# A one-core gated-attention and mixture-of-experts kernel: row weights travel with the scattered rows, expert 1 is split in phase one, and the mixing stage is rearranged

## What is computed

```python
x = x + layernorm(attention(layernorm(x)))        # state S = g_t * S + k_t v_t, y_t = q_t S
def swiglu(x, w1, w2, w3): h = x @ w1; return h * sigmoid(h) * (x @ w2) @ w3      # 256 -> 512 -> 256
gate_out = xn @ gate_w                            # 8 columns; top 2 are taken
w = softmax over the two largest, 0 elsewhere
out = sum_e swiglu(xn, ew1[e], ew2[e], ew3[e]) * w[:, e] + swiglu(xn, sw1, sw2, sw3)
x = x + layernorm(out)
```

## Time and profile before

| what | value |
|---|---|
| median of 3 runs (lowest, highest) | 833.86 us (831.44, 841.46) |
| the profiled execution's own time | 839.79 us |
| its span, first to last instruction | 837.9 us |
| mean granted PE clock | 0.953 |
| busy: PE, DVE, POOL, ACT | 87%, 66%, 61%, 49% |

### The profile page before, as it was taken

How to read it: one execution, slowest core, us unless ns; L and a number is a source line. 1 busy time by engine, 2 the same in 40 slices (tenths; PEclk the granted TensorE clock), 3 DMA queues, 4 the chain that set the end, 5 groups by cost and what they waited for, 6 DMA issues and landing times. The chain is left out here.

```text
span 837.9 us, 25066 instructions
## 1 busy us (share of the span) xinstructions
PE 732.9 (87%) x8863; PEld 609.9 (73%) x8863; DVE 551.6 (66%) x1130; ACT 408.4 (49%) x793; POOL 507.4 (61%) x672
## 2 busy tenths in 40 slices
PE   5889988898999878287999999999999999998970
PEld 4677776776877766165878999999999866887750
DVE  4999999888998886375777544444444434468852
ACT  3656655555666653222334444444444445445551
POOL 4133346776687676578098877886663444258864
PEclk9999999899999999587999999999999999999995
DMA  7435333443335433796212221212222122148864
GB/s 250 103 79 123 91 116 88 145 116 116 116 118 143 122 114 107 247 310 229 62 27 52 65 77 59 60 51 91 77 84 58 53 65 66 56 134 177 179 147 50
DMA packets 56934, 92.70 MB, mean 111 GB/s; under 512 B 7184, under 2 KB 35216, under 8 KB 56816
## 3 DMA queue, kind: packets, MB, share of 16 engines
q1 hardware_dynamic: 39424, 59.61, 25.4%
q0 software_dynamic: 11216, 23.10, 10.1%
q10 hardware_dynamic: 6176, 8.40, 3.1%
HBM read 59.07 MB, written 32.01 MB: 109 GB/s over the span
## 5 line engine op out<-in xcount | busy, mean ns | idle before, releaser
L1260 PE MATMUL bank<-xh,W 128*128 128x256 f16 x1504 | 261.8, 275 | 20.0 <-DVE gl L1556 13.8
L1260 PE MATMUL bank<-xl,W 128*128 128x256 f16 x752 | 206.8, 275 | 3.3 <-issue 3.3
L1260 PEld LDWEIGHTS bank<-xh,W 128*128 (+1 forms) x1504 | 148.2, 99 | 47.0 <-issue 16.7
L1301 PE MATMUL bank<-W,gh 128*128 (+1 forms) x824 | 142.3, 277 | 5.8 <-DVE gl L1556 3.9
L1339 ACT ACTIVATE gh<-bank 128x512 f16<-128x512 f32 x103 | 61.4, 596 | 160.8 <-DVE bank L1565 146.6
L1641 POOL DMA_INDIRECT yt_scratch<-ysh,dest x71 | 77.0, 1085 | 101.4 <-ACT ysh L1374 60.2
L1556 DVE TENSOR_TENSOR gl<-bank,gh 128x512 f16<-128x512 f32 x103 | 71.1, 691 | 73.0 <-ACT gh L1339 65.0
L1301 PE MATMUL bank<-W,gl 128*128 (+1 forms) x412 | 114.2, 277 | 0.0
L544 POOL DMA_INDIRECT xs_scratch<-xn_all,posi x64 | 92.9, 1451 | 27.5 <-issue 15.3
L1565 DVE SCALAR_TENSOR_TENSOR bank<-sl,w_scale,bank 128x512 f32<-128x512 f32 x94 | 70.9, 754 | 56.7 <-PE bank L1260 42.4
L596 PE MATMUL bank<-xnT,wT 128*128 128x256 f32 x384 | 93.6, 395 | 2.3 <-ACT xnT L371 2.3
(11 more groups left out here) (200 smaller groups left out, 1330.6 us busy)
## 6 DMA issues: line engine op xcount, KB each, us to landing
W<-gate_scratch SPq DMA_DIRECT2D x64, 256.0 KB
ysh<-yt_scratch SPq DMA_DIRECT2D x16, 512.0 KB, 4.4
xt<-xs_scratch SPq DMA_DIRECT2D x31, 260.0 KB
W<-in_L_ffn_ew_dram ACTq DMA_DIRECT2D x15, 512.0 KB, 3.8
W<-in_L_ffn_ew_dram SPq DMA_DIRECT2D x9, 512.0 KB, 9.1
x_in<-in_L_attn_x_dram SPq DMA_DIRECT2D x16, 256.0 KB, 4.0
out_dram<-x SPq DMA_DIRECT2D x16, 256.0 KB
xT_scratch<-xn2T SPq DMA_DIRECT2D x16, 256.0 KB
```

The source lines that it names most:

```text
L1260: last = mm(dst[n % 2][:, i * R:(i + 1) * R], W16[:, e, m, s, at:at + P], a[:, k, :], start=(k == 0 and s == 0 and a is x_h), stop=(k == K ...
L1301: last = mm(pYB[t.u % 2][:, r * D:(r + 1) * D], g[:, i, r, :], W16[:, e, 2, s, c * D:(c + 1) * D], start=(c == 0 and r == 0 and a is gh an ...
```

## The change

1. **Row weights.** `top` computes d per step, ACT's new `share` writes tanh(d / 2) into the fourth extra column, and POOL's `scatter` writes 0.5 - 0.5 tanh into the third. In phase two DVE's new `weights_of_rows` works out each loaded row's weight times the expert's scale, and `rows_out` evicts a routed tile with that as its scale, 256 columns at a time. `wts_all` and its computation go, and mixing becomes plain sums.
2. **Expert 1** is split by POOL in phase one in three pieces (`split_first`, steps i = 5 to 7, one matrix each), with two free `xn2` buffers as scratch.
3. **EARLY = 4**: one shared unit moves from the front to the back (routed units are 4 to 43, late shared ones 44 to 55). The table is spread over five gaps instead of three, and maxima and scales move two gaps later; `SHARE` stays.
4. ACT issues one load of an expert's matrix where it issued two.
5. **Last stage.** POOL makes the low part of late shared units' x. `add_first` is one sum of the two routed rows, `add_rows` one sum with the shared rows, behind the gated product; the normalisation moves one step later; three `lnc` buffers instead of two. The last two blocks read the shared result from PSUM; their residual is loaded by SP, added by DVE and stored by SP, without the accumulating transfer.
6. PE waits for evictions unit by unit (`rows_upto`), and projects the last singles ahead of the shared unit's hidden products.

```diff
-    EARLY = 5
+    EARLY = 4
...
+            def share(s):
+                act.wait_ge(s_dv, s + 1)
+                act.activation(xn2[s % XB][:, :, D + 3], dv[:, s], ACT.Tanh, scale=0.5).then_inc(s_share, 1)
...
             def scatter(s):
...
+                pool.wait_ge(s_share, s + 1)
                 pool.tensor_copy(xn2[s % XB][:, :, D:D + 2], tag_all[:, s]).then_inc(S["tag_ready"], 1)
-                need(pool, S["tag_ready"], s + 1)
+                pool.tensor_scalar(xn2[s % XB][:, :, D + 2], xn2[s % XB][:, :, D + 3], -0.5, 0.5, ALU.mult, ALU.add)\
+                    .then_inc(S["tag_ready"], 1)
+                need(pool, S["tag_ready"], 2 * (s + 1))
...
+            def split_first(m):
+                pool.wait_ge(s_scale, 1)
+                link(pool.tensor_scalar(spare_rows, W[:, 1, m, :], w_scale[:, 1, 1:2], 1.0, ALU.mult, ALU.mult))
+                link(pool.tensor_copy(W16[:, 1, m, 0, :], spare_rows))
+                last = pool.tensor_tensor(W16[:, 1, m, 1, :], spare_rows, W16[:, 1, m, 0, :], ALU.subtract)
...
                 on(residual, i - 2)
+                if 0 <= i - SPLIT - 1 < 3:
+                    split_first(i - SPLIT - 1)
...
+                V.tensor_tensor(dv[:, s], mx[:, s, :, 1], mx[:, s, :, 0], ALU.subtract).then_inc(s_dv, 1)
...
-                need(sp, U["mix2"], B * (c - 1))
+                need(sp, U["mix1"], c - 1)
...
+            def load_x1():
...
+                for c in PLAIN:
+                    sp.dma_start(x1_of[c], out_by_step[c]).then_inc(x1_loaded, 16)
+
+            def store_rows(c):
+                sp.wait_ge(U["sum_ready"], B * (c - PLAIN[0] + 1))
+                sp.dma_start(out_by_step[c], lnc[c % LN][:, :, :]).then_inc(last_stored, 16)
...
+                if t.routed:
+                    act.wait_ge(T["wrow_ready"], t.q + 1)
+                    for r in range(t.tiles):
+                        act.activation(ysh[:, ETILES + (t.j + r) % RING, :], pYB[t.u % 2][:, r * D:(r + 1) * D], ACT.Copy,
+                                       scale=wrow[:, t.j + r:t.j + r + 1]).then_inc(T["yo_ready"], 1)
...
-                need_dma(act, out_stored, c - 2)
+                need_dma(act, out_stored, c - LN)
...
+            TABLE = 5
...
-                turn = 3 * u + gap - 3
+                turn = 3 * u + gap - TABLE
...
+            def weights_of_rows(t, e):
...
+                dve.wait_ge(T["tag_ready"], 2 * (t.q + 1))
+                link(V.tensor_scalar(own, tag[:, t.j:t.j + t.tiles, 1], 0.0, None, ALU.is_equal))
+                link(V.tensor_tensor(part, own, x[:, 0:t.tiles, D + 3], ALU.mult))
+                link(V.tensor_tensor(part, part, x[:, 0:t.tiles, D + 2], ALU.add))
+                V.tensor_scalar(out, part, w_scale[:, 2, e], None, ALU.mult).then_inc(T["wrow_ready"], 1)
...
-                if following is not None:
+                if following is not None and u < MIX0:
                     low_x(following)
                 if prev is not None and prev.kind == "single":
                     low_g(prev, 0)
-                if steps:
-                    if steps[0] > 0:
-                        shift(steps[0] - 1)
-                    add_rows(steps[0])
+                if following is not None and following.routed:
+                    weights_of_rows(following, expert_of(dve, following))
+                if waiting is not None:
+                    shift(waiting)
                 beside(u, 0)
                 if t is not None:
                     e = expert_of(dve, t)
                     gated(t, 0, e)
                 if steps:
+                    add_rows(steps[0])
                     stats_of(steps[0])
...
+            for u in range(MIX0, ENDS):
+                if unit_at(u + 1) is not None:
+                    low_x(unit_at(u + 1))
+                for c in mixes[u]:
+                    add_first(c)
+                    if c > 0:
+                        rstd(c - 1)
+                    if c > 1:
+                        finish(c - 2)
             rstd(C - 1)
-            finish(C - 2)
-            finish(C - 1)
```

More of the change, by code:

```diff
@@ L462, in scalar_a @@
                 on(lambda s: mask_q(s, 1), i - 1)
-            act.wait_ge(s_dv, 1)
-            act.activation(ew[:, :], dv[:, :], ACT.Exp).then_inc(s_ew, 1)
         def pool_a(pool):
@@ L1132, in sandwich_kernel, with rows_upto @@
         tile_unit = {t.j + r: t for t in routed for r in range(t.tiles)}
+        def rows_upto(u):
+            return sum(t.tiles if t.routed else 1 for t in units[:u + 1])
         def halves_upto(u):
@@ L1154, in sandwich_kernel @@
         assert all(len(cs) in (1, 2) and c - EARLY + T0 + 2 <= u for u, cs in mixes.items() for c in cs)
+        PLAIN = (C - 2, C - 1)
+        x1_of = {c: xt[c % 2][:, :, 0:D] for c in PLAIN}
         def entry(eng, row, t, least, most):
@@ L1314, in tensor_b @@
                     turn_x(following)
+                late = [y for y in projected(u) if y.kind == "single" and t is not None and t.kind == "shared"]
+                for y in late:
+                    project(y, e_of.pop(y.u))
                 if t is not None:
@@ L1328, in tensor_b @@
                 for y in projected(u):
-                    project(y, e_of.pop(y.u))
+                    if y not in late:
+                        project(y, e_of.pop(y.u))
         def scalar_b(act):
@@ L1387, in load_matrices @@
             def load_matrices():
-                for e, m in [x for x in (next(matrices, None), next(matrices, None)) if x]:
+                e, m = next(matrices, (None, None))
+                if e is not None:
                     load_matrix(act, e, m)
@@ L1398, in scalar_b @@
                 t, prev, following = unit_at(u), unit_at(u - 1), unit_at(u + 1)
+                if following is not None and not following.routed:
+                    high_x(following)
                 for y in projected(u - 1):
-                    rows_out(y, e_of.pop(y.u))
+                    e = e_of.pop(y.u)
+                    if y.routed or y.n not in PLAIN:
+                        rows_out(y, e)
                 if following is not None:
-                    high_x(following)
                     e_of[u + 1] = expert_of(act, following)
                     if following.routed:
+                        high_x(following)
                         tags(following, e_of[u + 1])
                 load_matrices()
-                steps = mixes.get(u, ())
                 if t is not None:
@@ L1411, in scalar_b @@
                     high_g(prev, 0)
-                if steps and steps[0] > 0:
-                    normalise_rows(steps[0] - 1)
+                for c in mixes.get(u - 1, ()):
+                    normalise_rows(c)
                 if t is not None and t.halves == 2:
@@ L1646, in pool_b @@
             j = 0
-            for n, (first, end) in enumerate(GROUPS):
+            for n, (first, end) in list(enumerate(GROUPS))[1:]:
                 pool.wait_ge(s_scale, n + 1)
-                for e in range(max(first, 1), end):
+                for e in range(first, end):
                     split(e)
```

173 lines of the change are left out of this document (102 added, 71 removed).

## The result

The kernel after takes 878.07 us (median of 4 runs, 874.3 to 883.23), the kernel before, run beside it on the same chip, 835.82 us (4 runs, 831.44 to 841.46): ratio 1.0506, 95% interval 1.0413 to 1.0598. The prediction was 838.2 us with a range of 824 to 851; the kernel takes 40 us more. Ratios go by fast runs alone, which leaves two of the ten runs of experiment 11 out of its ratio. The profiled execution took 880.8 us (span 878.7), its counterpart before 839.8 (span 837.9).

What follows compares the result with a forecast made beforehand. DVE bounds phase one, PE the routed units at 8.30 us; +4.2 + 2.1 + 4.8 + 3.1 - 9.9 = +4.3 on 839.8 gives 844.1, carried to the median 838.2 us; range 824 to 851.

Steps and rivals of the forecast that it cites:

- the cost of the row weights in DVE's step: Routed units: four chained operations at 0.21 us and a second table read, 1.1 us a step on DVE.
- The second wait: Expert 2's first rows (fifth pair): later scales make PE wait 10 us, 45 us after the first routed rows; +2.1 us.
- Behind it: Units 7 to 9 take 10.3 us each while maxima ride, +4.8 us; then DVE's 8.0 stays under PE's 8.30.
- The signs that the prediction named for its own failure: No PE hole at expert 2's rows (forecast 10 too high), or phase one ending over 10 us later than 352 (too low).
- Phase one: Up to the handover: DVE's subtractions +2.7 and POOL's split pieces 1.5, together +4.2 us, bounds 0 and 21.
- Rival C: Phase one stretches: POOL's pieces and extra operation delay normalisations and hold DVE; 20.7 us, not 4.2, giving 855; chance 0.10.
- The start of the routed rows: First routed rows: expert 1's split no longer delays the load; rows at 396.3 us before phase one's share, instead of 407.37.
- Rival A: Expert 2 isn't waited for, as scales come before PE wants them; gives back 10 us, 828; chance 0.14.
- Rival D: PE's stop between 380 and 390 us belongs to the profiled execution only; the 5.9 us is lost, 844; chance 0.12.
- Late steps: Last stage: DVE's shift waits for POOL's queue ahead of the gated product; about 8.8 us a step, +3.1 us.
- Rival B: Last stage bound by PE, the shift never late: 69.3 us in place of 78.3, giving 829; chance 0.14.
- The tail: From the last eviction to the end: 10.1 us in place of 20.0, so -9.9 us.

Runs made afterwards that it cites:

- experiment 11: The kernel of experiment 9 with expert 1 split behind the pad scatters again, not in three pieces of phase one: 821.47 us, ratio 0.9917.
- Experiments 1 to 4: DVE's row weights left out of after (1.0185), moved to ACT (1.0196), kept with POOL's split in thirds (1.0301), added alone to before (1.0479).
- experiments 1 and 2: The kernel after with DVE's row weights left out (843.61 us), and with them formed on ACT (844.38 us).
- experiment 9: After with row weights on ACT, exchanges one unit later, three table gaps, five early units, and POOL forming the last stage's shift: 822.91 us, ratio 0.9942.
- experiment 10: The kernel of experiment 9 with the shift still on DVE, and the late shared units' low half of x back on DVE: 825.23 us, ratio 0.9968.

## Why the prediction was wrong, point by point

**The step that failed** is the cost of the row weights in DVE's step. "The second wait" has it as "four chained operations at 0.21", from the 171 ns of a copy, 1.1 us a unit with the table read, and "Behind it" goes on: "After that DVE's step, some 8.0 with the row weights, stays under PE's 8.30". Measured, the four take 11.7 us in the unit at 454.59, and 2.0 on average over 40 units. The steps behind the fifth pair, forecast at 10.3 and then 8.3, are 11.4, 21.9, 13.1, 11.3 and 12.8 us. I had the row that says otherwise on the table (3.42 us for a low part beside POOL's subtraction) and used it for phase one alone. But the new operations were put into the very units in which POOL splits experts 2 to 8, 34.6 us of 40 at the worst. Four chained operations meet POOL's instructions up to three times, 2.8, 2.7 and 6.0 us each. Experiments 1 to 4 show it from four sides: left out, moved, with shorter pieces, and alone. The signs that the prediction named for its own failure, no hole at the fifth pair or phase one over 10 us late, did not appear (there is a wait of 7.1 us, and phase one is 6.4 late): it looked for its error elsewhere.

The Trainium skill, "SBUF — State Buffer", section Who interferes with whom, says more than the sentence that I drew from it (GpSimd is its name for POOL): besides operations with two SBUF inputs, DVE's `tensor_scalar` can take the pair of ports that it shares with GpSimd, `tensor_reduce` never does, and ACT never waits. The trace agrees with each: 2.74 and 5.93 us for the two TENSOR_SCALARs, 1.21 for the reduction, 0.20 to 0.41 for one ACT operation.

**Phase one**, +4.2 predicted: its last row normalisation starts at 344.34 against 337.95, +6.4, within the bounds of 0 and 21. POOL's pieces did hold DVE there (DVE's own weight split took 2.29 us at 115.46 beside a piece's subtraction, and 1.19 at 141.59), and the seventh step's normalisation came 9.4 us late (181.2 against 171.8), but 3 us of it were given back. Rival C, phase one as the slow case, was the right mechanism in the wrong place.

**The start of the routed rows**: 400.5 with phase one's share, measured 401.7. The path of the load was right (issued at 396.89, 396.1 by the prediction), but PE waited only 1.1 us for it in this execution, not some 10; in experiments 1 and 2 it waited 6.9 and 5.6. The close agreement of the one number is in part luck. **The second wait**: the fifth pair 45 us later predicted, 43.7 measured, and a wait of 7.1 there where 10 was said. POOL waited 37.2 us for the scales, over 30 as said, and they came 29.0 us after the first routed rows (430.69 - 401.74) where 28.7 was said, so the path was right. No split ran on POOL until the scales came, so nothing held the new operations up to there. Missed was that SP's exchange also held the fourth pair's load, a smaller wait of 2.1 just ahead. Rival A is out, since there is a wait. Rival D, 6 us from PE's stop before the routed rows, wasn't tried. PE does 8.4 us of work from 380 to 390 in after and did 3.9 in before, so the stop isn't in every execution; 6 us are too little to explain 36.

**Late steps**: 8.8 predicted. ACT's evictions in after give two steps of 8.75 and two of 10.45, 9.6 on average:

```profile
800.02 0.68 ACT L1429 ACTIVATE ysh<-bank,w_scale 128x512 f32<-128x512 f32 x1
808.77 0.68 ACT L1429 ACTIVATE ysh<-bank,w_scale 128x512 f32<-128x512 f32 x1
819.21 0.68 ACT L1429 ACTIVATE ysh<-bank,w_scale 128x512 f32<-128x512 f32 x1
...
838.42 0.68 ACT L1429 ACTIVATE ysh<-bank,w_scale 128x512 f32<-128x512 f32 x1
```

The term was mis-sized by 4.0 us over the stage (+7.1 for +3.1). Two errors are known. The eight terms listed for a step add to 9.5, not to 8.8; with them the stage comes to 84.6 us and +9.4, so the figure of 8.8 isn't the sum that it is said to be. And I took shift and gated product at 0.95 where the shift alone takes 1.04 on average; the shift of 2.45 us above lies in a step of 10.45. The chain itself (POOL's queue, then shift, then product) is borne out by experiment 9, where taking the shift off DVE gains 6.5 us; experiment 10 doesn't contradict it. Rival B, PE-bound, is out, as the steps stand above 7.7. **The tail**: -8.9 for -9.9.

## What to carry over

Before placing a DVE operation of the kinds that were held here (two operands in SBUF, or a TENSOR_SCALAR from SBUF to SBUF), look at what POOL runs in that place. The price is set not by the size of the operation but by the length of POOL's instruction, and a chain can pay it more than once. Here it helped to move the operations to ACT, which took them at their plain cost, and, less, to cut POOL's long instructions in pieces. And a row that shows a mechanism holds for every part of the change, not only for the one under whose heading it was found.

## What the runs showed of the hardware

A DVE operation of two columns that starts in the 0.14 us between two POOL instructions passes at its 0.16 us (457.36); one that starts 0.12 us into the second waits until that ends (457.56, 2.64 us). It can wait out more than one: 2.42 us at 760.38 in experiment 9, over the rest of POOL's low half and its whole sum. POOL pays as well: in phase one of after, its operation on two columns that takes 0.23 us alone took 0.97 at 116.85 and ended with DVE's weight split (117.82 and 117.75).

PE's granted clock was 0.50, the lower of its two levels (1.2 GHz), from 444 to 448 us, behind the wait of 7.1 us, and again from 464 to 468, where PE stood still for DVE. The four transposes at 445.46 took 1.12 us where they take 0.60 at the higher level. So part of the loss there is PE at its lower clock behind the waits; how much, no run here separates.
